# Decoder stack on one core: projections of keys and values in a strand of their own, layer norms applied by another engine, a new order of steps

## The chip, the cores and the metric

The kernel runs on one core of one Trainium2 chip. The metric is the device time of one execution in microseconds, lower is better. Five engines work side by side, each through its own list of instructions in the order written: TensorE (PE in the profile), VectorE (DVE), ScalarE (ACT), GpSimd (POOL) and SyncE (SP), which here only issues transfers. They wait for each other by semaphores alone.

## The reference, cut to what matters

```python
x = _layernorm(x + _L0_attn_ref(x, ...))                 # gates and a linear recurrence over the 512 tokens
x = _layernorm(x + _L0_xattn_ref(x, ctx, ctx, ...))      # attention inside windows of 128, keys and values from ctx
x = _layernorm(x + _L0_ffn_ref(x, ...))                  # 256 -> 1024 -> 256, quantised weights plus LoRA
x = _layernorm(x + _L1_attn_ref(x, ...))                 # self-attention with clamped ALiBi bias
x = _layernorm(x + _L1_xattn_ref(x, ctx, ctx, group, mask, ...))  # keys and values from ctx, mask, weights multiplied by group
x = _layernorm(x + _L1_ffn_ref(x, ...))                  # causal attention with latent keys, then 8 experts, 2 per token
def _layernorm(x, eps=1e-05): return (x - mean(x)) / sqrt(var(x) + eps)
```

Four sequences of 512 tokens with 256 features, 16 heads of 16.

## The kernel before, in words

**Units.** One attention of one sequence is a unit `u`: units 0 to 3 are WINDOW, 4 to 7 ALIBI, 8 to 11 MASKED, 12 to 15 CAUSAL (`kind_of(u) = u // 4`, the sequence is `u % 4`). After the last unit come the experts in 46 tiles, and a final norm. A unit has four groups `g` of four heads.

**The steps of a unit.** Every step is a tuple such as `("QK", u, o, c)`. `TR` turns x to feature-major form `xt` (TensorE, copied by ScalarE). `QK` projects queries (o = 0) or keys (o = 1), half c of the features: TensorE multiplies, ScalarE writes a bf16 part (L1519), VectorE the rest (L1794, L1796). `SL` splits that rest again (ScalarE L1523, VectorE L1801): a float32 number is carried as three bf16 parts. `VP` projects the values into `va` (L1814). `OP(u, g, o)` moves parts of queries or keys with six transfers on SP's queue (L1038) into the operands `qs` and `ks`; a unit has four such steps, 24 transfers. `S` makes scores by query, VectorE takes their maxima (L1821, L1824, L1828), `P` splits the maxima, `M` turns them and SP writes them as three more operand rows (L1059). `T` makes scores by key, the maximum already subtracted in the product, and ScalarE takes the exponential (L1543). `E` multiplies by `group` on VectorE (MASKED only, L1855), `V` sums the values. `C` copies the result out: one transfer of the sums (L1064) and four of the heads (L1069). `R` (reciprocal, then a transfer, L1077) and `N` normalise, `OU` is the output projection with the residual.

**Norms.** `LS(b, n)` takes mean and variance on VectorE (L1752 to L1757) and has GpSimd raise to the power -0.5 (L1610). `LZ(b, n)` applies the norm: four VectorE instructions of 128x256, (x - mean) * rstd (L1767). There are 20 such pairs: n = 0 after the recurrence, 1 after WINDOW, 2 after the feed-forward, 3 after ALIBI, 4 after MASKED. `RS` and `RZ` are the RMS norms of the last layer, `FS` and `FZ` the final layer norm; these are applied by VectorE. `XB` adds an output bias to x on GpSimd (L1649).

**Who decides the order.** `streams()` lists the steps in strands; inside a strand the order is fixed. `plan()` merges the strands into one list `ORDER`: it takes over and over the strand head that could begin first, by costs per engine and waits in `parts_of()` (microseconds, written by hand) plus an offset per kind of step, `LAG`. `LAG` was found by a search over orders. Every engine then walks `ORDER` and emits its share, so a step's place in the list is its place in the queue of each engine, SP's too. `fill()` puts short products of constants (`WU`, L1164) into TensorE's gaps; they compute nothing that is used.

**Around the change.** In `streams()` the strand `before` holds for each unit recurrence or norm, `TR`, `XB`, then for c = 0, 1: `QK` of queries, `QK` of keys, `SL(u, c)`; then `VP`. So keys and values of WINDOW and MASKED units stand behind `TR`, though they come from the context `ct` alone. `rest` has one buffer per operand, and `SL(u, c)` splits queries and keys of half c in one instruction of 128x1024. Each transfer of `OP` is ready when `SL(u, g // 2)` is. In `parts_of()` a plain transfer costs SP 0.5, an `OP` 3.3, a `C` 2.5.

## Time and profile before

| | us |
|---|---|
| median of 3 runs | 1575.84 (1571.24 to 1581.65) |
| profiled execution, its own time | 1581.31 |
| its span, first to last instruction | 1579.3 |
| outside the span | 2.0 |
| TensorE busy | 1432.0 (91%) |
| VectorE busy | 1098.5 (70%) |
| ScalarE busy | 757.2 (48%) |
| GpSimd busy | 137.6 (9%) |

The profile's busy times are of one execution. Transfers are not counted as busy time of SP; the timeline shows them as SPq. A busy TensorE is not necessarily TensorE at its peak, since products overlap in it and their ends are modelled, and 55 us of it are the products of `fill()`. By the copies of finished heads (L1552) the WINDOW units end at 276.7 us, ALIBI at 675.8, MASKED at 1076.1, and CAUSAL at 1353.6.

### The profile page before, as it was taken

What the parts mean: (1) busy time and instruction counts of PE and PEld (TensorE: products, weight loads), DVE (VectorE), ACT (ScalarE), POOL (GpSimd) and SP (SyncE); (2) the same over time, 40 slices, a digit from 0 to 9 for tenths busy, and PEclk for the clock granted to TensorE, in tenths of its full rate; (3) what the DMA queues carried; (4) which work ended last, traced back from release to release, by engine and by line L of the source; (5) the groups of instructions that cost most, each with busy time, mean ns of one, the idle gap of its engine ahead of it and who ended that gap; (6) DMA issues with size and microseconds to landing.
All of it is one profiled execution on the core that took longest, in us unless ns stands there. A gap on an engine that the chain in (4) does not pass through costs nothing.

```text
span 1579.3 us, 29394 instructions
## 1 busy us (share of the span) xinstructions
PE 1432.0 (91%) x9731; PEld 805.2 (51%) x9764; DVE 1098.5 (70%) x2504; ACT 757.2 (48%) x1434; POOL 137.6 (9%) x126
## 2 busy tenths in 40 slices
PE   7788889999999999999999999999999959887990
PEld 3566565653654535343343343434455526777990
DVE  4897855673664667799999999997878845331523
ACT  4454644348346474645455444545565534322330
POOL 1001101100100100000000000000000030021304
PEclk7899999999999999999999999999999969998996
DMA  6332342302303221233222232021321252864862
GB/s 201 95 104 58 113 113 64 112 8 76 99 2 92 85 82 49 53 92 101 61 87 62 75 120 51 2 52 46 80 73 50 53 171 73 300 234 161 263 201 87
DMA packets 119345, 154.06 MB, mean 98 GB/s; under 512 B 31746, under 2 KB 99714, under 8 KB 117250
## 3 DMA queue, kind: packets, MB, share of 16 engines
q1 hardware_dynamic: 116132, 143.80, 30.7%
q0 software_dynamic: 3072, 8.39, 1.7%
q8 instruction: 87, 1.43, 0.4%
q14 instruction: 54, 0.44, 0.1%
HBM read 73.23 MB, written 18.35 MB: 58 GB/s over the span
## 4 chain that ended last, share of the span: by engine, by line
PE 71%; DVE 9%; issue 7%; SPq 6%; ACT 3%; DMA 2%; POOL 1%; DVEq 0%; POOLq 0%; ACTq 0%
PE ps L1132 24%; PE ps L1323 9%; PE ps L1360 6%; PE ps L1288 4%; SPq L1038 3%; PE ps L1283 3%; PE ps L1280 3%; PE ps L1351 3%; PE ps L1226 3%; PE ps L1355 2%; PE ps L1322 2%; PE ps L1290 2%; PE ps L1330 2%; DVE ps L1824 2%; ACT prob L1543 2%
## 5 line engine op out<-in xcount | busy, mean ns | idle before, releaser
L1543 ACT ACTIVATE prob<-ps 128x512 f32<-128x512 f32 (+3 forms) x832 | 407.3, 548 | 239.1 <-PE ps L1323 117.5
L1828 DVE TENSOR_REDUCE mx<-ps 128x1 f32<-128x512 f32 (+3 forms) x512 | 278.8, 584 | 108.4 <-PE ps L1290 51.4
L1323 PE MATMUL ps<-of_expert 99*128 99x512 bf16 (+4 forms) x768 | 253.3, 357 | 11.1 <-ACT prob L1543 4.5
L2000 DVE SCALAR_TENSOR_TENSOR room_b<-room_b,ps 128x512 f32<-128x512 f32 x46 | 31.6, 687 | 135.1 <-ACT room_b L1578 122.1
L1323 PEld LDWEIGHTS ps<-of_expert 99*128 99x128 bf16 (+1 forms) x768 | 73.4, 98 | 95.5 <-ACT prob L1543 42.3
L1610 POOL TENSOR_TENSOR rstd<-ve,half 128x4 f32<-128x4 f32 x28 | 31.3, 1118 | 1033.2 <-DVE ve L1757 744.6
L1360 PE MATMUL ps<-prob,va 128*32 128x512 f32 (+3 forms) x1024 | 115.7, 524 | 0.2
L1283 PE MATMUL ps<-of_expert 96*128 96x512 bf16 x256 | 89.4, 380 | 11.6 <-DVE mx L1824 9.5
L1288 PE MATMUL ps<-of_expert 102*128 102x512 bf16 x256 | 93.6, 382 | 1.5 <-issue 1.0
L1280 PE MATMUL ps<-of_expert 96*128 96x128 bf16 (+3 forms) x256 | 72.4, 307 | 18.4 <-issue 9.5
L1824 DVE CUSTOM_DVE_ANT_0 ps<-ps,room_a 128x512 f32<-128x512 f32 x128 | 85.7, 708 | 3.9 <-PE ps L1283 3.4
L1824 DVE CUSTOM_DVE_ANT_0 ps<-ps,room_b 128x512 f32<-128x512 f32 x128 | 85.7, 709 | 2.4 <-PE ps L1283 2.1
L1533 ACT ACTIVATE mrow<-ps 12x512 bf16<-12x512 bf16 x64 | 37.2, 582 | 91.7 <-PE ps L1304 91.5
L1132 PE MATMUL ps<-room_b,room_a 128*128 128x128 f32 x496 | 63.9, 284 | 18.2 <-issue 14.4
L1132 PE MATMUL ps<-xt,wa 128*128 128x512 f32 x160 | 77.7, 617 | 0.8 <-ACT xt L1493 0.8
L1855 DVE TENSOR_TENSOR room_h<-prob,room_b 128x1024 f32<-128x1024 f32 x64 | 76.7, 1218 | 2.1 <-ACT prob L1543 2.0
L1855 DVE TENSOR_TENSOR room_h<-prob,room_a 128x1024 f32<-128x1024 f32 x64 | 76.6, 1218 | 1.6 <-ACT prob L1543 1.6
L1283 PEld LDWEIGHTS ps<-of_expert 96*128 96x128 bf16 x256 | 22.0, 96 | 102.4 <-issue 99.4
L1132 PEld LDWEIGHTS ps<-room_b,room_a 128*128 128x128 f32 x496 | 62.2, 199 | 21.3 <-issue 16.1
L1132 PE MATMUL ps<-of_expert,room_b 128*128 x288 | 69.5, 385 | 1.0 <-DVE room_b L2000 0.5
L1351 PE MATMUL ps<-prob,ones 128*32 128x512 f32 x512 | 68.2, 604 | 0.0
L1355 PE MATMUL ps<-room_h,va 128*16 128x512 f32 x512 | 66.7, 592 | 0.0
(216 smaller groups left out, 2556.8 us busy)
## 6 DMA issues: line engine op xcount, KB each, us to landing
of_expert<-parts SPq DMA_DIRECT2D x384, 128.0 KB, 2.4
room_a<-in_w SPq DMA_DIRECT2D x38, 512.0 KB
room_b<-in_w SPq DMA_DIRECT2D x18, 512.0 KB
otc<-oraw SPq DMA_DIRECT2D x256, 32.0 KB, 2.0
sorted<-y SPq DMA_DIRECT2D x2, 2944.0 KB, 10.8
pack<-sorted SPq DMA_DIRECT2D x46, 128.0 KB
expert_out<-room_b SPq DMA_DIRECT2D x46, 128.0 KB
ct<-in_c SPq DMA_DIRECT2D x8, 512.0 KB, 4.3
```

Of the source, the lines that this page charges most:

```text
L1132: ins_ = pe.matmul(dst, lhs, rhs, start=(i == 0), stop=(i == len(lhs_rhs) - 1))
L1280: pe.matmul(dst[:, 0:(s + 1) * P], qs[0:rows, h, t], ks[0:rows, h, 0:(s + 1) * P], start=True, stop=False)
L1283: i = pe.matmul(dst, qs[0:rows, h, t], ks[0:rows, h, :], start=True, stop=True)
L1288: i = pe.matmul(dst, qs[0:rows, h, t], ks[0:rows, h, :], start=True, stop=not fix)
L1323: i = pe.matmul(dst[:, lo:S], ks[0:rows, h, t], qs[0:rows, h, lo:S], start=(a != MASKED), stop=(a != CAUSAL and not fixed))
L1351: pe.matmul(dst[32 * n:32 * n + 32, :], ones[:, :], prob[:, slot, n, :], start=begins, stop=False, tile_position=(0, 32 * n), skip_group_c ...
L1355: i = pe.matmul(dst[32 * n:32 * n + 16, :], v_in[:, s, J * g + n, 0:HD], weighed[:, QUAD_AT[st] % GROUPED, n, :], start=False, stop=ends, ...
L1360: i = pe.matmul(dst[32 * n:32 * n + 32, lo:S], v_in[:, s, J * g + n, :], prob[:, slot, n, lo:S], start=begins, stop=ends, tile_position=(0 ...
L1543: act.activation(prob[:, quad % PROBS, n, lo:S], key_bank(*st)[:, lo:S], ACT.Exp).then_inc(s_exp, 1)
L1824: i = dve.tensor_tensor_reduce(out=src, in0=src, in1=masks(seq_of(u))[0][:, s, :], scale=1.0, scalar=LOWEST, op0=ALU.add, op1=ALU.max, acc ...
L1828: i = dve.tensor_reduce(mx[:, slot, s, n:n + 1], src[:, 0:width], AX.X, ALU.max)
L1855: dve.tensor_tensor(weighed[:, quad % GROUPED, two, :], prob[:, quad % PROBS, two, :], masks(seq_of(u))[2][:, s:s + 1, :].to_broadcast([P, ...
```

## The change

Five things are done together.

1. A new strand `context` holds `QK` of the keys, `SL` of the keys and `VP` for WINDOW and MASKED units. The queries stay in `before`. In all units the keys come first as a whole, then the queries.
2. `SL(u, o)` now splits both halves of one operand, again as one instruction of 128x1024. `rest` doubles. `OP(u, g, o)` waits for `SL(u, o)` alone, and keys and queries have semaphores of their own.
3. `LZ` goes from VectorE to ScalarE as scale * x + shift, four instructions of 128x256. GpSimd makes the shift with two more small instructions for each norm. The next `LS` on the same buffers waits for this `LZ` on VectorE.
4. `va` is packed with 17 columns per head where it had 32. The products still read 32 columns, so rows 17 to 31 of each head's result now hold values of the next head, which nothing reads.
5. In `parts_of()` a transfer costs SP 0.6 where it cost 0.5, `OP` 3.7 (3.3), `C` 3.05 (2.5), `EW` 1.1 (1.0), a product 0.91 (0.92), and `LAG` comes from a new search. Nearly all its entries differ.

```diff
-        for c in range(NC):
-            before += [("QK", u, 0, c), ("QK", u, 1, c), ("SL", u, c)]
-        before += [("VP", u, 0), ("VP", u, 1)]
+        strand = context if a in (WINDOW, MASKED) else before
+        strand += [("QK", u, 1, 0), ("QK", u, 1, 1), ("SL", u, 1)]
+        if strand is before:
+            before += [("QK", u, 0, 0), ("QK", u, 0, 1), ("SL", u, 0)]
+        strand += [("VP", u, 0), ("VP", u, 1)]
+        if strand is context:
+            before += [("QK", u, 0, 0), ("QK", u, 0, 1), ("SL", u, 0)]
...
-        return [("DVE", 2.5, [src]), ("POOL", 1.0, [])]
+        return [("DVE", 2.5, [src]), ("POOL", 1.9, [])]
...
     if kind == "LZ":
         b, n = rest
-        return [("DVE", 1.7, [(("LS", b, n), "POOL")])]
+        return [("ACT", 1.6, [(("LS", b, n), "POOL")])]
...
-        return [("SP", 3.3, [(("SL", u, g // 2), "DVE")] + more, 2.0 * (last - g + 1))]
+        return [("SP", 3.7, [(("SL", u, o), "DVE")] + more, 2.0 * (last - g + 1))]
...
-                ("SP", 2.5, [(("OU", u - 1, 1), "PE")] if u else [], 0.6)]
+                ("SP", 3.05, [(("OU", u - 1, 1), "PE")] if u else [], 0.6)]
...
-        va = [sb(f"va{i}", [P, NT, H, 32]) for i in range(2)]
+
+        va = [sb(f"va{i}", [P, NT, H * (HD + 1) + 32 - HD - 1]) for i in range(2)]
...
-        rest = sb("rest", [P, NC, S])
+        rest = sb("rest", [P, 2, NC, S])
...
                 elif kind == "OP":
...
-                    sp.wait_ge(s_p2, nth("SL", u, g // 2))
+                    sp.wait_ge(s_p2, nth("SL", u, o))
...
+                elif kind == "LZ":
+                    b, n = st[1:]
+                    i_ = norm_buffer(n)
+                    act.wait_ge(s_rstd, nth("LS", b, n))
+                    for t in range(NT):
+                        i = act.activation(x[b][:, t, :], x[b][:, t, :], ACT.Identity, bias=shift[:, i_, t:t + 1], scale=rstd[:, i_, t:t + 1])
+                    i.then_inc(s_lnorm, 1)
...
                     elif u:
-                        act.wait_ge(s_qk, nth("QK", u - 1, 1, 1))
-                        act.wait_ge(s_vp, nth("VP", u - 1, 1))
+                        act.wait_ge(s_qk, nth("QK", u - 1, 0, 1))
+                        if kind_of(u - 1) in (ALIBI, CAUSAL):
+                            act.wait_ge(s_qk, nth("QK", u - 1, 1, 1))
+                            act.wait_ge(s_vp, nth("VP", u - 1, 1))
...
-                    act.activation(parts[:, :, 1, c, :], rest[:, :, :], ACT.Copy).then_inc(s_p1, 1)
+                    act.activation(parts[:, o, 1, :, :], rest[:, o, :, :], ACT.Copy).then_inc(s_p1, 1)
...
+                        pool.tensor_tensor(rstd[:, i_, :], ve[:, i_, :], half[:, :], ALU.pow).then_inc(s_g, mine.one())
+                        pool.wait_ge(s_g, mine.count)
+                        pool.tensor_tensor(shift[:, i_, :], mv[:, i_, :, 0], rstd[:, i_, :], ALU.mult).then_inc(s_g, mine.one())
+                        pool.wait_ge(s_g, mine.count)
+                        pool.tensor_scalar(shift[:, i_, :], shift[:, i_, :], -1.0, None, ALU.mult).then_inc(s_rstd, 1)
...
-                elif kind == "LZ":
-                    b, n = st[1:]
-                    i_ = norm_buffer(n)
-                    dve.wait_ge(s_rstd, nth("LS", b, n))
-                    for t in range(NT):
-                        i = dve.tensor_scalar(x[b][:, t, :], x[b][:, t, :], mv[:, i_, t, 0:1], rstd[:, i_, t:t + 1], ALU.subtract, ALU.mult)
-                    i.then_inc(s_norm, 1)
...
-                    dve.tensor_tensor(parts[:, :, 2, c, :], rest[:, :, :], parts[:, :, 1, c, :], ALU.subtract).then_inc(s_p2, 1)
+                    dve.tensor_tensor(parts[:, o, 2, :, :], rest[:, o, :, :], parts[:, o, 1, :, :], ALU.subtract).then_inc(s_p2, 1)
```

## Rows read from the trace of the kernel before

**Rows 1.** Stages in the windows view: stretch, its length, busy times, clock, DMA.
```profile
0.00:118.00 118.00, 90.27 (x692) 59.55 (x692) 87.43 (x160) 60.06 (x91) 12.16 (x17) 0.87 0.45 134
118.00:316.00 198.00, 181.81 (x1428) 122.09 (x1429) 135.62 (x299) 97.07 (x148) 22.16 (x14) 0.97 0.33 92
316.00:640.00 324.00, 319.66 (x1941) 161.02 (x1940) 204.72 (x418) 176.01 (x295) 15.50 (x10) 1.00 0.21 60
711.00:1066.00 355.00, 339.36 (x2037) 134.17 (x2068) 341.28 (x747) 175.87 (x309) 9.99 (x7) 1.00 0.24 68
1264.00:1310.00 46.00, 28.64 (x229) 16.91 (x222) 23.29 (x91) 12.71 (x33) 13.79 (x14) 0.70 0.47 148
```
**Rows 2.** The same view, instructions of L1164 (filling products) alone: PE, PEld.
```profile
0.00:118.00 118.00, 19.21 (x236) 17.25 (x236) 0.87 0.45 134
118.00:316.00 198.00, 4.42 (x59) 3.72 (x59) 0.97 0.33 92
1264.00:1310.00 46.00, 6.77 (x68) 5.54 (x68) 0.70 0.47 148
```
**Rows 3.** Shares by line of the chain that ended last, 80 to 120, 200 to 240 us.
```profile
by line: SPq L1038 39.1%; SPq L1069 14.4%; issue 9.6%; DMA of_expert<-mrow 8.1%; PE ps L1347 5.2%; SPq L1064 4.6%; DVE y L1702 3.1%; DVE room_a L1704 3.1%; SPq L1077 2.8%; PE ps L1278 2.7%; PE ps L1315 2.7%; SPq L1059 2.0%; DVE mx L1821 1.7
by line: SPq L1038 38.2%; SPq L1069 11.7%; PE ps L1137 6.8%; issue 6.1%; DMA of_expert<-mrow 5.5%; PE ps L1132 4.4%; PE ps L1315 4.2%; PE ps L1347 3.3%; ACT L1543 3.2%; DVE parts L1801 3.1%; SPq L1064 3.0%; SPq L1077 2.9%; ACT parts L1523 2
```
**Rows 4.** SP's queue in the timeline: start, length, line; x is the number of transfers.
```profile
44.95 16.32 SPq L1038 DMA_DIRECT2D of_expert<-parts  x24
89.10 7.71 SPq L1038 DMA_DIRECT2D of_expert<-parts  x12
1263.15 8.83 SPq L1038 DMA_DIRECT2D of_expert<-parts  x12
1272.68 2.74 SPq L1069 DMA_DIRECT2D otc<-oraw  x4
1275.48 0.81 SPq L1059 DMA_DIRECT2D of_expert<-mrow  x1
```
**Rows 5.** Norms applied and statistics in the groups by line; the first within 711 to 1066.
```profile
L1767 DVE TENSOR_SCALAR x<-x,mv,rstd 128x256 f32<-128x256 f32 x12 | 5.8, 548 | 0.0
L1767 DVE TENSOR_SCALAR x<-x,mv,rstd 128x256 f32<-128x256 f32 x80 | 32.6, 469 | 2.4 <-POOL rstd L1610 2.4
L1482 ACT ACTIVATE sq<-x 128x256 bf16<-128x256 f32 x16 | 6.6, 414 | 0.4
```
**Rows 6.** One norm in the timeline around 826 us, and one undisturbed.
```profile
827.15 1.92 POOL L1610 TENSOR_TENSOR rstd<-ve,half 128x4 f32<-128x4 f32 x1 [46.39 <-DVE ve L1757]
829.83 3.06 DVE L1767 TENSOR_SCALAR x<-x,mv,rstd 128x256 f32<-128x256 f32 x4
830.71 2.03 POOL L1649 TENSOR_TENSOR x<-x,pack 128x1024 f32<-128x1024 f32 x1 [1.64 <-PE ps L1137]
1029.48 1.38 DVE L1767 TENSOR_SCALAR x<-x,mv,rstd 128x256 f32<-128x256 f32 x4
```
**Rows 7.** GpSimd's smallest instructions and its power, from the groups by line.
```profile
L1610 POOL TENSOR_TENSOR rstd<-ve,half 128x4 f32<-128x4 f32 x28 | 31.3, 1118 | 1033.2 <-DVE ve L1757 744.6 <-DVE ve L1761 288.6
L1592 POOL MEMSET small<- 128x1 f32 x1 | 0.1, 110 | 0.0
```
**Rows 8.** Waits in two windows, 1264 to 1310 and 1415 to 1432 us: total, times, longest.
```profile
PE ps L1280 <- issue: 9.5, 5, 3.8
...
PE ps L1132 <- issue: 14.2, 1, 14.2
```
**Rows 9.** ScalarE's exponentials within 711 to 1066 us.
```profile
L1543 ACT ACTIVATE prob<-ps 128x512 f32<-128x512 f32 x226 | 122.2, 598 | 95.6 <-PE ps L1323 92.8
```

**Rows 10.** Copies of the last heads of the WINDOW, ALIBI and MASKED units, timeline.
```profile
276.68 0.60 ACT L1552 ACTIVATE oraw<-ps 128x512 f32<-128x512 f32 x1 [0.35 <-PE ps L1347]
675.81 0.60 ACT L1552 ACTIVATE oraw<-ps 128x512 f32<-128x512 f32 x1 [2.04 <-PE ps L1360]
1076.08 0.60 ACT L1552 ACTIVATE oraw<-ps 128x512 f32<-128x512 f32 x1 [3.47 <-PE ps L1355]
```

More of the change, by code:

```diff
@@ L238, in streams @@
     kept += [("EA", e) for e in range(NE)]
-    return [first, kept, added, normed, ops, turned, values, recips, normal, loads, outs, mask, weights, rows, before, later, routes, sums, grouped,
+    return [first, kept, added, normed, ops, turned, values, recips, normal, loads, outs, mask, weights, rows, context, before, later, routes, sums, grouped,
             keys, score, quant, ffn, experts]
@@ L348, in parts_of @@
         src = {(0, 1): ("LZ", b, 0), (1, 0): ("LZ", b, 1), (1, 1): ("LZ", b, 2), (2, 1): ("LZ", b, 3), (3, 1): ("RZ", b, 5)}[a, f]
-        xt = [(("VP", u - 1, 1), "PE")] if f and u else []
+        xt = [(("VP", u - 1, 1), "PE")] if f and u and kind_of(u - 1) not in (WINDOW, MASKED) else []
+        xt += [(("QK", u - 1, 0, 1), "PE")] if f and u else []
         if f == 0:
             xt = [(("UP", b - 1, NF - 1), "PE")] if b else [(("QZ", 1, 1), "DVE")]
-        return [("PE", 0.6, side + [(src, "DVE")]), ("ACT", 0.6, xt)]
+        return [("PE", 0.6, side + [(src, "DVE" if src[0] == "RZ" else "ACT")]), ("ACT", 0.6, xt)]
     if kind == "XB":
@@ L373, in parts_of @@
         a = kind_of(u)
-        more = [(("WS", a), "DVE")] + ([(("CL", u), "SP")] if o and u and a in (WINDOW, MASKED) else [])
+        more = [(("WS", a), "DVE")] if not o else [(("WL", a), "SP")] if a else loaded("wa", "pack")
+        more += [(("CL", u), "SP")] if o and u and a in (WINDOW, MASKED) else []
         more += loaded("ct") if o and not u else []
-        more += [(("LT", u), "ACT")] if o and a == CAUSAL else [(("TR", u, 1, 1), "ACT")]
+        more += [(("LT", u), "ACT")] if o and a == CAUSAL else [(("TR", u, 1, 1), "ACT")] if not o or a == ALIBI else []
         room = [(("OP", u - 1, piece_of(u - 1, g), o), "SP") for g in (2 * c, 2 * c + 1)] if u else []
@@ L880, in decoder @@
         s_alibi = [sem(f"alibi_of_quarter_{g}_loaded") for g in range(G)]
-        s_op = [sem(f"operands_of_quarter_{g}_loaded") for g in range(G)]
+        s_op = [[sem(f"{name}_of_quarter_{g}_loaded") for g in range(G)] for name in ("queries", "keys")]
         s_ml = [[sem(f"mask_{i}_of_{b}_loaded") for i in range(3)] for b in range(2)]
@@ L1270, in _ @@
                     rows = ALL_ROWS - 3 if a == ALIBI else ROWS
-                    pe.wait_ge(*op_ready(u, g))
+                    for o in range(2):
+                        pe.wait_ge(*op_ready(u, g, o))
                     if at >= len(S_BANKS):
@@ L1744, in _ @@
                     i_ = norm_buffer(n)
+                    before = norm_before(st)
+                    if before and before[0] == "LS":
+                        dve.wait_ge(s_lnorm, nth("LZ", *before[1:]))
                     if n == 0:
```

95 lines of the change are left out of this document (55 added, 40 removed), and 27 rows, old and new, of the table LAG.

## The prediction

> **What bounds the kernel now.** I read the busy times of the whole first, then the stages in the windows view, since an average of 91% for TensorE mixes stages with different limits. The reader is to see four kinds of stage in [rows 1]. From 316 to 640 us TensorE is busy 319.66 of 324 us, and VectorE and ScalarE have slack. From 711 to 1066, the MASKED attention, VectorE is busy 341.28 of 355 us, 96%. TensorE seems full there too (339.36), but it is fed by VectorE's buffers, so its busy time is stretched. In the first 316 us no engine is full: TensorE is idle for 27.7 + 16.2 = 43.9 us, and 19.21 + 4.42 = 23.6 us of what looks busy are filling products [rows 1, 2]. That makes 67.5 us in which it has nothing useful to do. From 1264 to 1310 it is idle 17.4 us, with 6.8 us of filling.
>
> Then I read the chain that ended last, for what the open time waits on. Between 80 and 120 us 39.1% + 14.4% + 4.6% + 2.8% + 2.0% = 62.9% of the chain are SP's transfer issues, some 25 us of 40, and between 200 and 240 us 38.2% + 11.7% + 3.0% + 2.9% = 55.8%, some 22 us [rows 3]. The timeline says why. Twelve operand transfers take 7.71 to 8.83 us of SP, 24 take 16.32 us, so 0.64 to 0.74 us each [rows 4]. The planner before reckoned 3.3 us for six, 0.55 each. Whatever is queued behind such a block comes late. At 1263.15 twelve transfers are issued, then the heads of a finished group, and only at 1275.48 the row of maxima, for which the exponentials wait [rows 4].
>
> **Layer norms to ScalarE.** In the stretch that VectorE bounds there are 12 instructions of L1767, 5.8 us together. They go from the engine that decides. The other 17 groups, most of the 32.6 us, lie where VectorE has slack and are worth nothing by themselves [rows 5]. What comes instead is 80 ScalarE instructions. The nearest row, a square of 128x256, takes 414 ns [rows 5], so a norm costs ScalarE 1.66 us and three of them 5.0 us in that stretch, beside a ScalarE that is busy 175.87 of 355 and whose exponentials sat 92.8 us waiting for TensorE's scores [rows 1, 9]. That cover is wide. Without it each norm would hold back an exponential, TensorE's next score by key, and the weighing on VectorE, and the 5.0 us would come back. I take -5, between -9 (a norm or two more at the ends of the stretch, where VectorE is nearly full) and 0.
>
> GpSimd gets two more instructions for each norm. None like them is in the trace: below they are bounded by the smallest row, 0.11 us, above by the power, 1.12 us [rows 7]. A norm becomes ready 0.2 to 2.2 us later. I take 0.7, nearer to the small row since they multiply four numbers per partition. GpSimd is busy 9.99 of 355 us, so only the latency counts, and it counts where the next unit waits for its norm, which is in the WINDOW units, with four to eight norms: +3 us, between 0 and +12. VectorE's new wait in `LS` mostly finds its predecessor done, since 20 norms are spread over more than 1000 us; 0, at most +2.
>
> VectorE's norm at 829.83 took 3.06 us, against 1.38 us at 1029.48; a GpSimd addition of 2.03 us ran beside it [rows 6]. So the two engines hinder each other here. The Trainium skill ("SBUF — State Buffer", on engine ports and contention) states that the two share a port pair as an exclusive lock, which the loser waits out whole. The trace agrees as far as VectorE loses to GpSimd. It speaks for taking the norm away (the disturbed ones go) and against the two new GpSimd instructions, which could block VectorE in its turn: by the rule with the upper price, three norms of two locks would put back up to 6 x 1.12 = 6.7 us, and the sum would be -14 in place of -19; by the row of the power at 827.15, which itself grew to 1.92 us while VectorE worked on, GpSimd loses and VectorE does not.
>
> **Keys, values and queries apart.** The amount of work stays: 32 `SL` pairs of 128x1024 before and after, as many products and transfers. What moves is the place. A WINDOW unit's keys need only the context and the weights, so twelve of its 24 transfers can be issued while recurrence, norm and turning are still on their way. Before, all 24 stood behind the queries. In the first unit the 16.32 us block [rows 4] then has only 12 transfers, about 7.7 us, behind the queries. VectorE is busy there too, with quantising weights, and takes part of this away. I take -4 for the first unit and -4 for each of the two later places where the chain runs through SP [rows 3], -12 in all. The bounds are 0 (if the recurrence or VectorE is late in SP's place) and -25, half of the 47 us of SP time on the chain in rows 3. Against it: the queries' transfers of the first piece now wait for both halves of the queries, and in ALIBI and CAUSAL units the first `OP` waits for all four projections where it waited for two. An ALIBI unit lasts 399.1 / 4 = 100 us [rows 10], and half of it lies between operands ready and operands needed, which hides that. In the WINDOW units it can cost the two products and a split, some 2 us a unit, and is inside the range.
>
> **The order with dearer transfers.** The planner now reckons 0.62 us for a transfer of `OP` and 0.61 for one of `C`, near what [rows 4] show, so blocks such as the one at 1263.15 can be seen by it and laid elsewhere. There 8.83 + 2.74 us and one more issue stand ahead of the maxima. But TensorE had other work for a part, and of the 17.4 + 6.8 us open in this stretch 9.5 are waits marked issue, in which TensorE waited for nothing that the profile shows, like the 14.2 us near 1415 [rows 8]. An order of steps has no hold on these that I can see. I take -5, between +5 and -15: the order is new everywhere, and can lose somewhere what it wins.
>
> **At nothing:** the packed `va`, since its products have the same shapes and VectorE writes as many elements; the new semaphores; SP's prices for the experts, where TensorE is full until 1540 us.
>
> **Sum:** -5 + 3 - 12 - 5 = -19 us. The profiled execution took 1581.3 us (span 1579.3 and 2.0 around it), 5.5 above the median of the runs shown, so it becomes 1562 by its own measure and 1557 by the median. A measurement of this kernel can tell about 1% from no change, 1560.1 us and below.
>
> **Rivals.** (a) SP's transfers were on the chain only by name: VectorE's quantising, the recurrence and the projections would have ended soon after, and something else is late in their place. For it: VectorE is busy 87.43 of the first 118 us. Against it: 67.5 us without useful work for TensorE. Only VectorE's relief of 5 us stays: 1571.
>
> (b) Both places and more go whole: half of rows 3's 47 us (-24), 7 from the norms (their upper half), and -9 from the hole at 1264. That is -40: 1536. For it: the whole order was wrong about transfers by 15 to 35%, so small losses of this kind should stand all along. Against it: in the 324 us of ALIBI there are only 4.3 us to win on TensorE.
>
> (c) Slower: ScalarE works in order, and a norm now waits there for VectorE's statistics and three GpSimd instructions with the exponentials queued behind it. With only three buffers of key scores TensorE stops soon after. The price is 1.66 us of work and up to 2.2 us of waiting for each of 20 norms, 77 us if nothing hides it. It decides once more than 1 us a norm is exposed beyond what is won, as 20 norms x 2 us = 40 us against 19 us won: +21, 1597. For it: the planner's 1.9 us on GpSimd is an unmeasured number. Against it: ScalarE is half idle in every stage.
>
> (d) That the change does not do what it says I hold for impossible in the norms, which are named instructions; for the context strand it would be rival (a).
>
> **How the numbers follow.** The forecast (-12 to -30, so 1546 to 1564) has 0.42, rival (a) 0.29, (b) 0.16, (c) 0.13. Faster by over 1% means -16 or better: 0.70 of the forecast's own case, all of (b), none of (a) beyond a little, in sum 0.47. Slower by over 1%, above 1591.6: 0.09, two thirds of (c). The rest, 0.44, is within 1%. The range reaches from (b) to a little past (a): 1534 to 1586.
>
> **What would show it.** L1767's successor appears on ScalarE 80 times at 0.38 to 0.42 us, and VectorE's busy time falls by some 32 us. The MASKED units, 400.3 us from 675.8 to 1076.1 [rows 10], take 392 to 396. The first twelve transfers of the first unit are issued before its queries are ready, and the WINDOW units end near 265 where they ended at 276.7 [rows 10]. The chain between 80 and 240 us holds half as much SPq. The forecast is wrong if the WINDOW end has not moved (then (a)), or if the ALIBI units take longer than their 399.1 us between ends [rows 10] because TensorE waits for exponentials (then (c)).

## The result, with the profile after

Median of 19 runs each: 1583.47 us after the change (1579.59 to 1593.17) and 1579.04 before. The ratio is 1.0042, with a 95% interval of 1.0028 to 1.0056, so by the ratio the changed kernel is slower by 6.6 us (the two medians lie 4.4 us apart). The forecast was 1557, a gain of 19 us. The profiled execution took 1583.40 us (span 1581.6), and the one before 1581.31 (span 1579.3).

The stages of the profile after, in the windows view, as [rows 1] (length, then busy time of PE, PEld, DVE, ACT, POOL, clock, DMA share, GB/s):

```profile
0.00:118.00 118.00, 90.99 (x643) 57.61 (x643) 83.58 (x137) 62.31 (x97) 11.77 (x20) 0.94 0.42 125
118.00:316.00 198.00, 187.59 (x1435) 124.70 (x1431) 118.47 (x271) 117.52 (x184) 26.80 (x32) 0.99 0.31 83
316.00:640.00 324.00, 317.00 (x1981) 158.49 (x1979) 210.69 (x409) 183.14 (x312) 16.50 (x17) 1.00 0.25 70
711.00:1066.00 355.00, 343.04 (x2195) 135.78 (x2196) 339.84 (x740) 181.96 (x326) 10.11 (x12) 1.00 0.22 64
1264.00:1310.00 46.00, 27.42 (x245) 14.81 (x244) 26.43 (x95) 11.55 (x28) 15.74 (x16) 0.78 0.47 157
```

and the filling products alone (L1182, before L1164 [rows 2]):

```profile
0.00:118.00 118.00, 15.83 (x199) 14.11 (x199) 0.94 0.42 125
118.00:316.00 198.00, 6.24 (x88) 5.34 (x88) 0.99 0.31 83
```

In the first 316 us TensorE's time without useful work was 67.5 us. It is now (118 - 90.99 + 15.83) + (198 - 187.59 + 6.24) = 59.5 us. The copies of the last heads, as [rows 10], do not show that gain:

```profile
279.27 0.60 ACT L1583 ACTIVATE oraw<-ps 128x512 f32<-128x512 f32 x1 [0.35 <-PE ps L1369]
678.27 0.60 ACT L1583 ACTIVATE oraw<-ps 128x512 f32<-128x512 f32 x1 [1.13 <-PE ps L1382]
1073.58 0.60 ACT L1583 ACTIVATE oraw<-ps 128x512 f32<-128x512 f32 x1 [1.01 <-PE ps L1377]
```

WINDOW ends 2.6 us later, not 12 earlier. ALIBI lasts 399.0 us (before 399.1), MASKED 395.3 (before 400.3). The chain that ended last has lost its SP part, as forecast. Shares by line from 80 to 120 and from 200 to 240 us, as [rows 3]:

```profile
by line: SPq L1056 15.5%; PE ps L1210 7.8%; PE ps L1150 7.7%; PE ps L1369 6.2%; DVE y L1739 6.0%; SPq L1087 5.8%; DMA of_expert<-mrow 5.7%; issue 5.5%; ACT room_b L1471 3.9%; PE ps L1337 3.3%; DVE mx L1856 3.3%; ACT L1574 3.2%; DVE y L1741 
by line: PE ps L1150 56.5%; PE ps L1244 18.2%; PE ps L1369 7.4%; PE ps L1337 4.5%; PE ps L1300 4.2%; PE ps L1155 3.4%; DVE va L1849 1.9%; ACT xt L1524 1.5%; ACT y L1524 1.5%; issue 0.7%; PE ps L1326 0.7%
```

SP's issues (SPq) held some 25 and 22 us of these stretches. The two leading ones now have 21.3% of 40 us, some 9 us, and in the second stretch TensorE has some 95% of it. So the time left SP and stayed in the kernel.

Two things are needed to read what follows. **The table of stages.** For each profile the copies of the last heads give the end of WINDOW and the lengths of ALIBI, MASKED, the first three CAUSAL units, and the rest of the span:

```
                               WINDOW  ALIBI  MASKED  CAUSAL 1-3  rest   span
before                          276.7  399.1  400.3   188.2      315.0  1579.3
before again (e6)               274.2  399.1  399.4   188.2      313.2  1574.1
after                           279.3  399.0  395.3   192.9      315.1  1581.6
after again (e7)                281.3  398.8  395.6   192.4      313.1  1581.2
after, third (e17)              282.5  399.4  395.3   191.6      320.0  1588.8
e1  order before, norms ScalarE 275.6  410.5  400.9   189.8      285.2  1562.1
e2  order after, norms VectorE  286.9  404.2  400.3   194.9      278.8  1565.1
e3  before + 96 SP transfers    330.0  398.7  399.5   188.3      283.9  1600.5
e4  after + 96 SP transfers     335.0  399.2  395.3   191.2      279.8  1600.5
e5  before, stores paced        274.0  398.8  399.5   188.2      303.8  1564.2
e8  before, keys by GpSimd      269.4  403.0  400.1   188.4      319.2  1580.1
e9  after, stores paced         280.6  399.7  395.4   192.5      301.1  1569.2
e10 after, no shift             281.8  399.6  395.5   191.0      315.4  1583.3
e11 before, four in flight      273.9  399.2  400.4   188.3      304.2  1566.0
e12 e5 and e8 together          268.2  402.8  400.7   188.3      300.9  1560.9
e13 before + TensorE in MASKED  271.8  399.2  401.5   188.5      281.3  1542.2
e14 before + TensorE in ALIBI   268.2  405.1  399.6   188.3      282.4  1543.6
e15 before + VectorE in MASKED  273.5  399.0  399.6   188.3      285.2  1545.6
e16 e5 again                    275.4  399.3  399.9   188.2      297.3  1560.1
e18 e5, third                   275.6  399.0  399.8   188.3      301.7  1564.4
```

The kernel before took 1576 to 1579 us in the session of the result and in four of the six later ones, and about 1546 in the other two, one of these on a chip that showed 1577 in another session. The table says where: in the rest, 313 to 315 against 281 to 285 us; ALIBI, MASKED and CAUSAL 1-3 of this order agree within 1.0 us where no edit touches them. Ratios are therefore taken within a session only. e1 to e4 and e13 to e15 are of the quick sessions. The changed kernel as it stands was never run in one, so that it loses 0.4% there too is not shown.

**The open time.** Busy time alone hides filling, so for each stage I take length - PE busy + filling: the time in which TensorE did nothing useful. What is left of the stage is useful work. WINDOW, MASKED and CAUSAL 1-3, before:

```profile
0.00:276.70 276.70, 234.40 (x1873) 155.18 (x1874) 195.42 (x403) 143.53 (x223) 29.35 (x28) 0.92 0.38 107
675.80:1076.10 400.30, 383.48 (x2298) 153.44 (x2331) 382.12 (x839) 196.72 (x347) 13.47 (x9) 1.00 0.25 70
1076.10:1264.30 188.20, 182.01 (x1470) 97.18 (x1469) 146.93 (x376) 112.13 (x280) 5.04 (x5) 1.00 0.24 61
```

its filling (L1164), and the same two views after (L1182):

```profile
0.00:276.70 276.70, 23.18 (x290) 20.64 (x290) 0.92 0.38 107
675.80:1076.10 400.30, 16.42 (x212) 13.84 (x212) 1.00 0.25 70
1076.10:1264.30 188.20, 5.12 (x63) 3.92 (x63) 1.00 0.24 61
```

```profile
0.00:279.30 279.30, 242.53 (x1904) 161.34 (x1905) 182.44 (x367) 161.51 (x257) 32.89 (x46) 0.97 0.36 102
678.30:1073.60 395.30, 380.68 (x2400) 154.36 (x2400) 375.62 (x820) 203.33 (x361) 14.62 (x16) 1.00 0.24 69
1073.60:1266.50 192.90, 184.51 (x1497) 98.77 (x1495) 145.66 (x385) 114.30 (x286) 5.97 (x7) 0.99 0.24 60
```

```profile
0.00:279.30 279.30, 22.07 (x287) 19.45 (x287) 0.97 0.36 102
678.30:1073.60 395.30, 21.06 (x301) 18.87 (x301) 1.00 0.24 69
1073.60:1266.50 192.90, 6.67 (x93) 5.57 (x93) 0.99 0.24 60
```

Open in WINDOW: 276.7 - 234.40 + 23.18 = 65.5 before, 279.3 - 242.53 + 22.07 = 58.8 after. Useful work by its end: 211.2 before, 220.5 after. Open in MASKED: 33.2 and 35.7; in CAUSAL 1-3: 11.3 and 15.1. In words: the change did win 6.7 us of TensorE's time in WINDOW, but not as an earlier end. Its order has eight `DN` and one `UP` steps more ahead of WINDOW's last copy, against two `VP` and six `S` steps fewer. At ALIBI's end the lead is two `VP`, one `QK` and two `TR` steps, less two `S`, and at MASKED's end there is next to none. The lead came back out of MASKED: useful work in that stage fell from 400.3 - 33.2 = 367.1 to 395.3 - 35.7 = 359.6 us, and the stage became only 5.0 us shorter. Useful work over the whole is the same, 1432.0 - 55.2 = 1376.8 and 1434.5 - 58.3 = 1376.2.

### The profile page after: what moved, and what is told of

It reads as the page before. It is cut to its first block, busy times and chain, and to the rows that moved or that the text cites. A ratio compares the mean times of both kernels' runs of the same rounds, so it can differ in the third digit from the quotient of the medians.

```text
span 1581.6 us, 29693 instructions
## 1 busy us (share of the span) xinstructions
PE 1434.5 (91%) x9861; PEld 805.6 (51%) x9861; DVE 1073.0 (68%) x2424; ACT 796.6 (50%) x1514; POOL 145.9 (9%) x166
## 4 chain that ended last, share of the span: by engine, by line
PE 64%; DVE 14%; issue 8%; SPq 5%; ACT 4%; DMA 3%; POOL 1%; another core or an unknown queue 0%; DVEq 0%; POOLq 0%; ACTq 0%
PE ps L1150 22%; PE ps L1345 8%; PE ps L1382 6%; PE ps L1310 4%; DVE ps L1859 3%; PE ps L1302 3%; PE ps L1305 3%; PE ps L1244 3%; PE ps L1373 2%; SPq L1056 2%; PE ps L1344 2%; PE ps L1377 2%; PE ps L1352 2%; PE ps L1312 2%; DVE room_h L1890 2%
## 5 line engine op out<-in xcount | busy, mean ns | idle before, releaser
L1609 ACT ACTIVATE room_b<-ps 128x512 f32<-128x512 f32 x46 | 27.5, 597 | 88.2 <-PE ps L1150 71.2
```

## The experiments

**Order and engine, each alone.**

> The kernel before, its order of steps held to the letter; only the 20 layer norms are applied by ScalarE, with GpSimd's two extra instructions. Theory A (the norms' move is sound, the new order loses what it won): the VectorE-bound MASKED stretch gets shorter by 3 to 5 us, the WINDOW units lose 1 to 3, in sum 0 to 4 us faster than before. Theory B (the norms' move is the loss, since a norm takes ScalarE 2.06 us where 1.66 was reckoned, and is ready 0.7 us later, with exponentials behind it): 20 x 2 us exposed in part, 4 to 20 us slower than before.

> The changed kernel, its order held; only the norms go back to VectorE and GpSimd's two extra instructions go. Against before, the changed kernel itself stands at 1.0042. Theory A: 2 to 6 us slower than the changed kernel, ratio 1.006 to 1.008, since VectorE gets the norms back in the MASKED stretch. Theory B: faster than the changed kernel by 4 us or more, ratio 1.002 or lower.

```diff
--- e1: order of before, norms moved (e2 is the reverse, on the changed order)
-FAMILY = {"RS": "LS", "RZ": "LZ", "FS": "LS", "FZ": "LZ"}
+FAMILY = {"RS": "LS", "FS": "LS", "FZ": "RZ"}
...
+                elif kind == "LZ":                       # ScalarE
+                    act.wait_ge(s_rstd, nth("LS", b, n))
+                    for t in range(NT):
+                        i = act.activation(x[b][:, t, :], x[b][:, t, :], ACT.Identity, bias=shift[:, i_, t:t + 1], scale=rstd[:, i_, t:t + 1])
...
+                        pool.tensor_tensor(shift[:, i_, :], mv[:, i_, :, 0], rstd[:, i_, :], ALU.mult).then_inc(s_g, mine.one())
+                        pool.wait_ge(s_g, mine.count)
+                        pool.tensor_scalar(shift[:, i_, :], shift[:, i_, :], -1.0, None, ALU.mult).then_inc(s_rstd, 1)
```

e1: 1565.94 us, ratio 1.0137 (1.0116 to 1.0157), 21 us, at the upper end of its theory B and a little beyond. e2: 1573.20, ratio 1.0181 (1.0164 to 1.0198), worse than either of its theories. Both are worse than before, and by the end of CAUSAL 1-3 worse than the changed kernel. The table places it: e1 loses 11.4 us in ALIBI, and MASKED stays at 400.9. What TensorE waited for in ALIBI, before and in e1 (us in total, times, longest):

```profile
PE ps L1323 <- ACT prob L1543: 3.0, 6, 1.0
PE ps L1132 <- ACT y L1493: 1.1, 1, 1.1
```

```profile
PE ps L1326 <- ACT prob L1553: 6.1, 9, 1.6
PE ps L1135 <- ACT y L1503: 5.5, 2, 3.0
```

These are the exponentials and the turned norm, both ScalarE's: the mechanism of rival (c). Together these waits grew by 7.5 us of the 11.4. With the changed order it does not occur. e2 says what the norms on ScalarE are worth in that order: with them on VectorE WINDOW is 4 to 8 us longer, ALIBI 5, MASKED 5, CAUSAL 2 to 4. So at the end of CAUSAL 1-3 the move costs 13 to 16 us in one order (1276.9 against 1260.4 to 1264.3) and saves 18 to 20 in the other (1286.3 against 1266.5 to 1268.8). A price such as my -5 for the move alone doesn't exist.

The same holds for the open time of WINDOW. For e2, and its filling (L1182):

```profile
0.00:286.90 286.90, 239.72 (x1904) 161.37 (x1905) 189.82 (x399) 145.61 (x225) 27.45 (x28) 0.93 0.35 99
0.00:286.90 286.90, 20.22 (x287) 17.55 (x287) 0.93 0.35 99
```

That is 286.9 - 239.72 + 20.22 = 67.4 us open, and the same sum gives 66.9 for e1, where before has 65.5 and the five profiles of the changed order with norms on ScalarE 58.8 to 61.0. With the norms on VectorE, the strand of keys and the new order won none of it.

**What SP's time is worth.**

> The kernel before with one more small transfer (2 KB to a spare buffer) behind each operand transfer of the four WINDOW units: 96 more on SP, some 0.6 us each, 14 to 15 us per unit. The output is the same. If SP's issue time bounds the WINDOW units, as the chain said (25.7 + 22.4 us of it in 80 us), the time rises by half of 58 us or more, 25 to 58. If SP was on the chain only by name, by less than 10.

> The same dose in the changed kernel. If the new strand and order freed the WINDOW units from SP, the rise over the changed kernel is less than half of the rise in the kernel before. If they only renamed the wait, the rise is the same within 5 us.

```diff
                         sp.dma_start(dst[slot:ROWS:len(slots), heads, :], ...
+                        if u < NB:
+                            sp.dma_start(spare[((u * G + g) * 2 + o) * 6 + slot], half[:, :]).then_inc(s_spare, 16)
```

e3: 1601.17 us, ratio 1.0356 (1.0336 to 1.0377). e4: 1600.50, ratio 1.0340 (1.0318 to 1.0363). WINDOW ends at 330.0 and 335.0, some 55 and 54 us later than the means of the two orders (274.9 and 281.1). The dose is 96 issues of about 0.58 us, 56 us: nearly all of it counts in both kernels. So SP was on the path in truth when it becomes dearer, and the changed order has not taken it off. With the dose the two kernels are equal (0.9996 of each other) in a quick session: e4 is 4.1 us behind at the end of CAUSAL 1-3 and makes it good in the rest.

> The kernel before, order held; the keys' operand transfers of the four WINDOW units, 48 in all, are issued by GpSimd, so SP has some 31 us less to issue there. If SP bounds the WINDOW units also from below (taking away wins as adding costs, slope 0.6 to 1), these units end 10 to 25 us sooner and the time falls by as much. If SP's share can be taken away without a win, since VectorE and the recurrence are as late, they end within 4 us of 276.7.

```diff
-                elif kind == "OP":
+                elif kind == "OP" and not (kind_of(st[1]) == WINDOW and st[3] == 1):
...
-                    pe.wait_ge(*op_ready(u, g))
+                    for need in op_ready(u, g):
+                        pe.wait_ge(*need)
...
+                elif kind == "OP" and (kind_of(st[1]) == WINDOW and st[3] == 1):
...
+                        pool.dma_start(dst[slot:ROWS:len(slots), heads, :], parts[rows, o, slots[slot], g // 2, :]).then_inc(s_opg[g], 16)
```

e8: 1579.91 us, ratio 1.0019 (1.0002 to 1.0035). Half of SP's operand transfers in WINDOW are off its queue, and this is what is left of it at the ends of WINDOW and ALIBI:

```profile
269.42 0.60 ACT L1557 ACTIVATE oraw<-ps 128x512 f32<-128x512 f32 x1 [0.35 <-PE ps L1351]
672.39 0.60 ACT L1557 ACTIVATE oraw<-ps 128x512 f32<-128x512 f32 x1 [2.04 <-PE ps L1364]
```

Against e6, the kernel before in the same session, WINDOW ends 4.8 us earlier and ALIBI 0.9. WINDOW ends of the unchanged order scatter from 268.2 to 276.7, but its open time does not: 63.3 to 65.7 us in nine profiles, and 60.4 in e8 (59.4 in e12 below). The relief is real, 4 to 5 us of some 31 us taken off SP, and WINDOW's end lies between its two expectations. It is gone 400 us later, but that is no sign that ALIBI swallows a lead: the edit makes TensorE wait for two semaphores before every `S` step where it waited for one. The idle time before the weight loads of these steps in ALIBI, in the groups by line of e6 and e8:

```profile
L1288 PEld LDWEIGHTS ps<-of_expert 102*128 102x128 bf16 x249 | 23.3, 97 | 47.3 <-issue 41.4
L1292 PEld LDWEIGHTS ps<-of_expert 102*128 102x128 bf16 x249 | 23.3, 97 | 52.4 <-issue 46.8
```

That is 5.4 us more marked issue, in a stage in which TensorE has only 8 to 10 us open. A lead that no edit pays for is kept: the profile of before ended WINDOW 2.5 us after e6, ALIBI 2.6 and CAUSAL 1-3 3.4 after. So SP's time is worth itself upwards, and downwards about a sixth at WINDOW's end; what of that would reach the end of the kernel, e8 cannot tell, and an edit without the second wait was not run.

> e5 and e8 together: the kernel before, sorting stores paced, and the 48 key transfers of the WINDOW units issued by GpSimd. If the 5 us won at the end of the WINDOW stage are swallowed by the ALIBI stage whatever comes later: WINDOW ends at 269, ALIBI at 671 to 673, and the time is that of e5, ratio 0.991 to 0.994. If they were swallowed in e8 by chance of the holes near 1285: ratio 0.989 or less.

e12 (the edits of e5 and e8): 1564.32 us, ratio 0.9929 (0.9904 to 0.9954), that of e5. ALIBI is 402.8 again, and the idle time marked issue before the same weight loads is 46.9 us (41.8 in e5). So the loss of e8's gain has nothing to do with what comes after 1265 us.

**Where TensorE's and VectorE's time counts.**

> The kernel before with seven more filler products (128 by 128, 0.09 us each) on TensorE at the start of every head quarter's value product in the MASKED units: 16 by 0.62 us, 10 us more TensorE work in that stage and nowhere else. Theory (MASKED is bound by VectorE and the order, so TensorE work taken out of it comes back as filler): the stage grows from 400 by 0 to 4 us, ratio 1.000 to 1.003. Rival (TensorE time is worth itself everywhere): +10 us, ratio 1.006.

> The same 10 us of filler products, in the ALIBI units instead. Theory (ALIBI is bound by TensorE, 1.6 us of filler and 6.9 idle in 399): the stage grows by 8 to 10 us, and since it is followed by stages that do not make up for it, the time too: ratio 1.005 to 1.006. Rival (there is room in it after all): ratio 1.002 or less.

> The kernel before with four more small VectorE instructions (128 by 4, some 0.16 us each) behind the reciprocals of every head quarter of the MASKED units: 16 by 0.64 us, 10 us more VectorE work in that stage. Theory (VectorE is its bound, busy 382 of 400 us): the stage grows by 8 to 10 us, ratio 1.005 to 1.006; that is the reverse of what the norms taken off VectorE gave (4 norms, 6.5 us less busy, 5.0 us less stage). Rival (the order paces it, not VectorE): +0 to 3, ratio 1.002 or less.

```diff
+                    if a == MASKED and s == 0:                               # e13; e14: a == ALIBI
+                        for _ in range(7):
+                            pe.matmul(dst[:, 0:P], identb, identb, start=True, stop=True)
...
+                    if kind_of(u) == MASKED:                                 # e15, VectorE, after the reciprocals
+                        dve.wait_ge(s_v, mine.count)
+                        for i in range(4):
+                            dve.tensor_scalar(spare[:, i, :], ones[:, 0:4], 1.0, None, ALU.mult).then_inc(s_v, mine.one())
```

The doses were smaller than meant. TensorE's 112 products in e14, in the windows view of L1344, and VectorE's 64 instructions in e15, in the groups by line:

```profile
268.00:674.00 406.00, 8.86 (x112) 7.39 (x112) 1.00 0.23 64
```

```profile
L1866 DVE TENSOR_SCALAR spare<-ones 128x4 f32<-128x4 f32 x64 | 5.0, 147 | 0.0
```

So 8.9 and 5.0 us. e13: ratio 1.0009 (0.9995 to 1.0024), 1.4 us for 8.9, and MASKED is 1 to 2 us longer. e15: 0.9993 (0.9980 to 1.0006), nothing for 5.0, and MASKED is as before. e14: 1.0023 (1.0008 to 1.0038), 3.6 us for 8.9, and ALIBI takes 405.1 us, 6 more than the 398.7 to 399.4 that this order takes without an edit there. e14's WINDOW ended 3.6 and 5.3 us before those of e13 and e15, which its edit does not touch; but the loss in ALIBI is no jump behind that end. It grows by some 0.4 us with nearly every group of heads, each of which has one dose of 0.55 us. The last copies of WINDOW and of the four ALIBI units:

```
e14                268.2   407.9   525.1   598.8   673.3
e15                273.5   411.5   527.1   599.7   672.5
e14 minus e15       -5.3    -3.6    -2.0    -1.0    +0.8
```

I had expected 8 to 10 us in ALIBI and in e15. In ALIBI two thirds of the dose came in the stage: there TensorE is the bound, nearly. In MASKED neither came: with TensorE and VectorE each showing 96% busy, 5 to 9 us more on either cost almost nothing. That also prices the pulled-forward work, since it came back out of MASKED: at 0.16 us per us (1.4 for 8.9), the 9 to 12 us of it are worth 1 to 2, and by the end of the interval (3.7 for 8.9) no more than 5. This is an estimate: a cost of added work is used for a gain from work removed.

**The chain through GpSimd.**

> The changed kernel with the mean left out of the layer norms: the shift is zero, so GpSimd's two short instructions and their latency (1.04 + 0.22 + 0.36 us against 1.04) are gone from all 20 norms, and ScalarE waits 0.6 us less for each. The rest of the instructions are the same. If the chain from statistics to the applied norm is what eats the gain in the ALIBI stage: 20 norms by 0.6 to 0.9 us, 12 to 18 us less, ratio below 0.996, and the ALIBI stage falls from 399 to under 393. If it is ScalarE's own time (2.06 us per norm) or the order: within 3 us of the changed kernel, ratio 1.002 to 1.005.

```diff
+            pool.memset(shift[:, :, :], 0.0).then_inc(s_g, mine.one())
...
-                        pool.tensor_tensor(rstd[:, i_, :], ve[:, i_, :], half[:, :], ALU.pow).then_inc(s_g, mine.one())
-                        pool.wait_ge(s_g, mine.count)
-                        pool.tensor_tensor(shift[:, i_, :], mv[:, i_, :, 0], rstd[:, i_, :], ALU.mult).then_inc(s_g, mine.one())
-                        pool.wait_ge(s_g, mine.count)
-                        pool.tensor_scalar(shift[:, i_, :], shift[:, i_, :], -1.0, None, ALU.mult).then_inc(s_rstd, 1)
...
+                    pool.tensor_tensor(rstd[:, i_, :], ve[:, i_, :], half[:, :], ALU.pow).then_inc(s_rstd, 1)
```

e10, which leaves the mean out of the 20 norms: 1586.02 us, ratio 1.0066 (1.0049 to 1.0083), not below the changed kernel. The two instructions and their latency cost nothing that can be measured. My +3 for them is refuted.

**The pause behind the sorting stores.** In both kernels TensorE waits for nothing that the profile shows, near 1285 and near 1415 us. After, in the windows 1264 to 1310 and 1415 to 1432, as [rows 8]:

```profile
PE ps L1302 <- issue: 11.0, 6, 5.2
PE ps L1150 <- issue: 14.0, 1, 14.0
```

GpSimd issues 16 indirect stores there back to back. Before, in GpSimd's timeline:

```profile
1278.90 1.31 POOL L1621 DMA_INDIRECT sorted<-room_h,place  x1 [49.47 <-issue]
1280.51 0.96 POOL L1621 DMA_INDIRECT sorted<-room_h,place  x1 [0.30 <-issue]
1281.78 0.96 POOL L1621 DMA_INDIRECT sorted<-room_h,place  x1 [0.31 <-issue]
...
```

> The kernel before, order held; GpSimd's 32 scattering transfers, which go out in two blocks of 16 at 1.27 us each, now have at most two on their way (each waits for the one two places before). If the waits of all engines marked issue or remote near 1285 and 1415 us (9.5 and 14.2 us on TensorE) come from these blocks crowding out the loading of instructions, they shrink and the time falls by 5 to 20 us. If they come from something else, the time stays within 3 us or rises by up to 15, since a batch's first tile waits longer.

```diff
+                    for half_ in range(2):                                   # SP, before it fetches a tile's rows
+                        sp.wait_ge(s_sx[k][half_], 16 * NT * len(BATCHES[k]))
...
                     for j in range(2):                                       # GpSimd
+                        sent = NT * BATCHES[k].index(b) + t
+                        if sent:
+                            pool.wait_ge(s_sx[k][j], 16 * sent)
                         pool.indirect_dma_start(xs[k][:, :], ...
-                                                None).then_inc(s_sx[k], 16)
+                                                None).then_inc(s_sx[k][j], 16)
```

e5: 1565.89 us, ratio 0.9923 (0.9905 to 0.9941). The stores now wait for each other, and TensorE works through both holes (28.64 of the first 46 us busy before [rows 1]):

```profile
1276.66 0.96 POOL L1625 DMA_INDIRECT sorted<-room_h,place  x1 [0.30 <-issue]
1281.12 0.96 POOL L1625 DMA_INDIRECT sorted<-room_h,place  x1 [3.50 <-DMA sorted<-room_h,place]
1282.38 0.96 POOL L1625 DMA_INDIRECT sorted<-room_h,place  x1 [0.30 <-issue]
...
```

```profile
1264.00:1310.00 46.00, 35.42 (x309) 20.07 (x306) 29.74 (x98) 18.00 (x49) 17.02 (x17) 0.93 0.44 141
1415.00:1432.00 17.00, 15.77 (x103) 14.08 (x101) 2.75 (x4) 4.74 (x11) 7.67 (x8) 1.00 0.52 184
```

> The kernel before with at most four sorting stores of a batch in flight, instead of two as in e5 or no bound. If the stall is that of a full queue behind sixteen stores, four are as good as two: ratio 0.992. If the stall grows with every store beyond those in flight: between e5 and before, ratio about 0.995 to 0.998, with PE waits without a named releaser of 3 to 8 us near 1285 and 1415.

e11: 1565.13 us, ratio 0.9924 (0.9908 to 0.9941), as good as two in flight. (In it every tile of the experts fetches the rows of tile 3 in place of its own; the number and size of the transfers are the same.) Waits without a releaser are 11.3 us between 1240 and 1460, where e5 has 1.6 but waits 11.0 us for sorted rows that land later: the sum is what counts, and it is equal.

> The changed kernel with at most two of the 32 sorting stores of a batch in flight, the same edit as in e5. Theory (the holes at 1265-1305 and 1408-1430 are the stores' and belong to both kernels alike): it loses what before lost, 12 us, and reads ratio 0.996 to the kernel before, about 1571, still some 5 us over e5 (0.992); the issue waits of 11.0 and 14.0 us on TensorE go. Rival (the changed order stands worse against the holes, its expert tiles being left over because of them): paced, it falls by 16 us or more and stands level with e5, ratio 0.992 or less. Second rival (the sorting stores cost the changed kernel nothing on the path): it stays at 1.004.

e9: 1573.63 us, ratio 0.9979 (0.9959 to 0.9999). Against its own ratio of 1.0042 the changed kernel wins 10 us by pacing, as before wins 12, and stays 8.8 us behind e5. So the pause belongs to both alike and hides nothing of the difference.

**Repeats.**

> The kernel before, unchanged, for a trace of it on the chip of these runs, which is 2% quicker than that of the first profile if it is the one of the last experiments (1545.6 against 1579.0 us). Every theory expects the same ends of stages up to MASKED within 1 us (276.7, 675.8, 1076.1). If the chips differ in how instructions reach the engines, the gap is all in the 45 us around 1280 and in the experts' stretch; if they differ in clock or transfers, it is spread over all stages.

> The changed kernel, unchanged. Both theories: ratio 1.000 to 1.008 to the kernel before on this chip too. If the ratio is clearly different from 1.004, part of the first result belongs to the places where a chip stalls and not to the change.

> e5 unchanged, in another session. The kernel before took 1577 us in two of the four sessions so far and 1546 in the other two, once on the same chip, and profiles of the quicker ones show no wait without a releaser near 1285 and 1415. Theory (the pause is the sorting stores' in some sessions only, and pacing trades it for a later landing of the stores): where before takes about 1577, ratio 0.992; where it takes about 1547, pacing has nothing to win and its own cost remains, 1550 to 1565, ratio 1.002 to 1.012. Rival (pacing frees something in either): below 0.997 in both.

> The changed kernel again, in the same session as e16. Where before takes about 1577: ratio 1.004. Where before takes about 1547: the stages up to 1265 us are the same, with CAUSAL 4.7 us longer and MASKED 5.0 shorter, so the ratio stays at 1.001 to 1.006; if the pauses had hidden a gain or a loss of the changed order in the expert part, it is outside of that, on either side.

> e5 unchanged, once more. Only of use in a session in which before takes about 1547: there, if pacing costs what the later landing of the stores costs, ratio 1.002 to 1.012; if the quicker sessions and pacing are alike, 0.998 to 1.002. In a session in which before takes about 1577: 0.989 to 0.993 again.

e6 took 1576.13 us in its one run, the stages as before and 313.2 us for the rest. e7: 1582.90, ratio 1.0039 (1.0024 to 1.0054). e17: 1590.97, ratio 1.0077 (1.0054 to 1.0099), more than its expectation in a session of 1577; its WINDOW is the longest of the five of this kernel and its rest 5 us longer, with one wait of TensorE for VectorE of 8.7 us inside the first hole. e16: 1561.30, ratio 0.9891 (0.9862 to 0.9920). e18: 1564.60, ratio 0.9923 (0.9905 to 0.9940). Pacing has won 0.7 to 1.1% in four sessions (e12 with them), all with the pause. What pacing does in a quick session, without the pause, was not measured and is open. e3 and e4 stand for the two orders in a quick one: from the end of CAUSAL's third unit on they take 283.9 and 279.8 us, of which 1 to 3 us are work that the changed order had done earlier. Put beside the 6 us by which the changed order is late at that point, this makes its loss in a quick session 2 us or so, an estimate from two profiles.

## Why the prediction was wrong

**Where the 6.6 us are.** Over the profiles with the changed order (after, e7, e9, e10, e17) and those with the old one in the same kind of session (before, e6, e5, e11, e16, e18) the means are: WINDOW 281.1 against 274.9, +6.1; ALIBI 399.3 and 399.1, +0.2; MASKED 395.4 and 399.9, -4.4; CAUSAL 1-3 192.1 and 188.2, +3.8. That is +5.7 of the 6.6; the rest of the kernel differs by less than it scatters.

**The bound, right in its figures and wrong in its use.** The open 67.5 us existed and fell to 59.5. But "VectorE is the engine that decides" in MASKED, read from 96% busy, failed as a statement on load: 5.0 us more of VectorE work there cost nothing (e15). e1 says the same: with the norms taken off VectorE and nothing else changed, MASKED stayed at 400.9. That a norm counts there as a link of a chain, and not as load, fits this but was not shown by itself.

**Norms, -5 in MASKED: right in size, -4.4, and in part by luck.** MASKED lost these 4.4 to 5.0 us only where the norms' move and the new order came together: e1 has 400.9 and e2 400.3. Two terms were mis-sized. ScalarE takes 591 ns for each instruction, 2.06 us for a norm, not 1.66, and it sat idle 16.1 us before the norms, waiting for the shift. GpSimd's two instructions take 0.22 + 0.36 us, near the 0.7 taken. From the groups by line of the profile after:

```profile
L1510 ACT ACTIVATE x<-x,shift,rstd 128x256 f32<-128x256 f32 x80 | 41.3, 591 | 16.1 <-POOL shift L1649 16.1
L1645 POOL TENSOR_TENSOR rstd<-ve,half 128x4 f32<-128x4 f32 x20 | 20.7, 1037 | 495.5 <-DVE ve L1799 495.5
L1649 POOL TENSOR_SCALAR shift<-shift 128x4 f32<-128x4 f32 x20 | 7.2, 360 | 1.8
L1647 POOL TENSOR_TENSOR shift<-mv,rstd 128x4 f32<-128x4 f32 x20 | 4.5, 223 | 1.6
```

The trace of before held ScalarE's price, in two forms of one line that differ by one operand per partition. Its groups by line:

```profile
L1519 ACT ACTIVATE parts<-ps 128x512 bf16<-128x512 f32 x16 | 9.6, 597 | 19.2 <-PE ps L1132 19.2
L1519 ACT ACTIVATE parts<-ps,pack 128x512 bf16<-128x512 f32 x24 | 16.5, 687 | 27.2 <-PE ps L1132 27.0
```

That operand adds 90 ns, and the norm has two, scale and shift: 414 + 180 = 594. The square that I took as the nearest row has none. The Trainium skill states the same ("ScalarE: Activation LUTs", on what a table load costs): some 93 ns for each such operand. The trace agrees; I had not read either for this.

GpSimd's latency costs nothing (e10). The rule of the Trainium skill on the port pair ("SBUF — State Buffer") would have put back up to 6.7 us; the -4.4 leaves no room for that. (My sum by that rule was wrong, too: -19 and 6.7 make -12, not -14.) Where the engines met GpSimd lost, not VectorE: its last instruction took 1.07 us at 709.43, 812.10 and 907.78, in three of the four norms around MASKED, where it takes 0.23 to 0.27 undisturbed, and the VectorE instruction beside it at 811.83 took 1.26 us, where its kind takes 1.21 to 1.24 on average. What the step missed is that the sign hangs on the order: +13 to +16 us by the end of CAUSAL 1-3 in the old one (e1), -18 to -20 in the new (e2). Rival (c)'s mechanism was true in the old order, its price near what e1 shows (ratio 1.0137 is 21 us); in the new order ALIBI did not grow.

**Keys apart, -12: the step that failed.** I took SP's issues on the chain for the wait that the open time hangs on, and 12 us of them for time that the kernel would get back. The chain lost its SP, as I said, and the time did not fall: downwards SP was on the chain mostly by name, as rival (a) has it. In the first unit the keys' products were done early, but the last part of their split is VectorE's, and VectorE was reducing weights for the quantising (L1724), the risk that I had named and priced too low:

```profile
37.00 0.75 DVE L1831 SCALAR_TENSOR_TENSOR rest<-ps,pack,parts 128x512 f32<-128x512 f32 x1 [0.96 <-ACT parts L1550]
37.66 4.47 DVE L1724 TENSOR_REDUCE small<-room_a 128x1 f32<-128x2048 f32 x2
42.05 1.22 DVE L1836 TENSOR_TENSOR parts<-rest,parts 128x1024 bf16<-128x1024 f32 x1
43.29 18.56 SPq L1056 DMA_DIRECT2D of_expert<-parts  x24
```

The first transfer leaves at 43.29 us where it left at 44.95 [rows 4], and all 24 still go in one block. With the norms on VectorE the strand and its order won no open time at all (e2, 67.4 us), and taking some 31 us off SP in the old order won 4 to 5 (e8, e12). Only together with the norms' move 4 to 7 us of open time were won over WINDOW, a third to a little over a half of the -12. WINDOW ended 6.1 us later all the same, because the changed order had TensorE do 9 to 12 us more of other work before it, and that work came back out of MASKED, where 8.9 us of TensorE's time are worth 1.4 (e13). What the strand does without the new order was not tried.

**The order, -5: wrong in sign.** It costs +3.8 us in CAUSAL 1-3, where open time grew from 11.3 to 15.1. e2 (194.9, norms on VectorE) shows that this comes with the order; the norms' move alone accounts for 1.6 at most (e1, 189.8). Which step of it is at fault was not tried and stays open. That the order has no hold on the waits without releaser was right (11.0 and 14.0 us are still there), but they were no fate: they hang on how densely the sorting stores are issued.

**Of the signs listed** two came as said: MASKED within 392 to 396, and SPq on the chain more than halved. VectorE's busy time fell by 25.5 us (1098.5 to 1073.0), not 32. The instructions on ScalarE are 0.59 us, the keys' transfers did not go ahead, and WINDOW did not end near 265. By the text's own test, a WINDOW end that has not moved to 265, rival (a) is the nearest; it said 1571, and by e2 and the table what is left to 1583 goes with the new order, whose parts were not tried one by one.

## What to carry to other kernels

Time saved on a queue that leads the chain is a gain only if the next wait is shorter too: try it in both directions, a dose and a relief, since the two can differ widely (56 us for 56 us put on, 4 to 5 for some 31 us taken off). Look at what the edit of such an experiment costs by itself: here one more semaphore wait before each score step can account for all of the relief that was lost. When an engine assignment and a searched order change together, measure all four combinations; by the end of CAUSAL 1-3, where the sessions agree, each half alone costs 13 to 16 and 22 to 26 us here, and the two together 6. And look at waits that the profile cannot name: the only gain of this study, 0.7 to 1.1%, came from bounding how many indirect stores are in flight.

## What the runs showed of the hardware

GpSimd's multiplications of 128x4 take 0.22 and 0.36 us on average, where the power takes 1.04. A second semaphore wait on TensorE before each score step of ALIBI came with 5.4 us more idle time marked issue over 249 weight loads (e8 against e6), some 0.02 us each. Sixteen indirect stores issued 1.27 us apart go with pauses of TensorE of 10 + 14 us in some sessions and none in others, on the same chip (chip 9: 1576.69 us for the kernel before in one session, 1547.27 in another). With two in flight the waits without a releaser shrink to 1.6 us (e5), with four to 11.3 (e11), and either way 12 us are won, 17 in e16. So in the sessions with the pause it needs the dense stores; what else it needs, and by what they cause it, was not tried.
